# First layer with transposed probabilities and row-wise evidence; squares and feed-forward evacuations on VectorE

## The reference

```
# layer 0, for each of the 16 batches
nx       = layer_norm(x, gamma, beta)                  # 56 x 128
scores   = (nx @ Wq) @ (ctx @ Wk).T * 128 ** -0.5      # 56 x 1500
weights  = softmax(scores)
evidence = weights @ (ctx @ Wv)                        # 56 x 128
combined = [nx, evidence, anchor] -> router, 3 experts, gate -> x = x + delta

# layers 1 to 3: norm -> 16-head attention over the 1500 context rows -> projection
# layers 2 and 3: also self-attention, and h = gelu(norm(x) @ W1 + b1); x = x + h @ W2 + b2
```

## Time and profile before

| what | us |
|---|---|
| median of 3 runs | 1776.51 (1770.99 to 1777.41) |
| profiled execution, its own time | 1769.27 |
| its span, first to last instruction | 1767.5 |
| PE busy | 1562.3 (88%) |
| PEld busy | 996.4 (56%) |
| DVE busy | 1164.7 (66%) |
| ACT busy | 976.2 (55%) |
| POOL busy | 659.8 (37%) |

### The profile page before, as it was taken

How to read it: one execution, slowest core, us unless ns; L and a number is a source line. 1 busy time by engine, 2 the same in 40 slices (tenths; PEclk the granted TensorE clock), 3 DMA queues, 4 the chain that set the end, 5 groups by cost and what they waited for, 6 DMA issues and landing times.

```text
span 1767.5 us, 49986 instructions
## 1 busy us (share of the span) xinstructions
PE 1562.3 (88%) x20479; PEld 996.4 (56%) x20479; DVE 1164.7 (66%) x2425; ACT 976.2 (55%) x1878; POOL 659.8 (37%) x898
## 2 busy tenths in 40 slices
PE   7999977499999998887999999988887999899886
PEld 5667733166666665543566666655443566566554
DVE  3555455577777777366777777764557777777572
ACT  2333323077777677332567776764332677676663
POOL 4000074146666643446366665610332222222110
PEclk9889889599999999798799999997897999999897
DMA  8444214145665544024355655432033466666520
GB/s 240 125 138 145 84 45 95 40 120 133 159 164 152 133 110 116 1 71 109 82 143 152 161 148 147 116 94 47 1 71 93 120 150 160 156 155 146 124 62 6
DMA packets 193275, 199.49 MB, mean 113 GB/s; under 512 B 58949, under 2 KB 182536, under 8 KB 193048
## 3 DMA queue, kind: packets, MB, share of 16 engines
q1 hardware_dynamic: 191464, 195.22, 43.6%
q10 hardware_dynamic: 1008, 1.05, 0.2%
q0 software_dynamic: 576, 0.02, 0.0%
HBM read 114.46 MB, written 72.17 MB: 106 GB/s over the span
## 4 chain that ended last, share of the span: by engine, by line
PE 69%; DVE 13%; ACT 11%; issue 4%; DMA 2%; POOL 1%; SPq 1%; DVEq 0%; ACTq 0%; POOLq 0%
PE PS L1414 14%; PE PS L1242 9%; PE PS L1440 8%; PE PS L1235 7%; PE PS L1388 5%; DVE mx L1881 4%; ACT q_parts L1009 3%; PE PS L1178 3%; PE PS L1188 3%; PE PS L1516 3%; PE PS L1195 3%; ACT v_sb L918 2%; PE PS L1229 2%; PE PS L1089 2%; PE PS L1426 2%
## 5 line engine op out<-in xcount | busy, mean ns | idle before, releaser
L1881 DVE TENSOR_REDUCE mx<-PS 112x1 f32<-112x500 f32 x1152 | 713.5, 672 | 213.3 <-PE PS L1388 211.3
L1009 ACT ACTIVATE q_parts<-PS 125x448 f32<-125x448 f32 x1152 | 562.0, 543 | 159.3 <-PE PS L1440 151.5
L741 POOL CAST k_hi<-k_full 128x500 f16<-128x500 f32 x144 | 89.0, 618 | 631.3 <-issue 556.7
L1440 PEld LDWEIGHTS PS<-q_st,k_st 50*125 50x125 f16 x4608 | 183.5, 137 | 232.1 <-ACT q_parts L1009 162.6
L776 POOL TENSOR_SCALAR cx<-cx,norm_b 125x128 f32<-125x128 f32 x384 | 306.7, 814 | 19.8 <-issue 15.9
L1440 PE MATMUL PS<-q_st,k_st 50*125 50x112 f16 x4608 | 258.7, 233 | 41.5 <-ACT q_parts L1009 32.3
L1414 PE MATMUL PS<-q_parts,v_sb 125*18 125x112 f32 x9216 | 289.0, 268 | 0.0
L1414 PEld LDWEIGHTS PS<-q_parts,v_sb 125*18 125x18 f32 x9216 | 216.3, 100 | 53.2 <-issue 41.3
L1388 PE MATMUL PS<-k_st,q_mx 50*112 50x500 f16 x1080 | 225.2, 384 | 7.6 <-DVE mx L1881 5.2
L743 POOL TENSOR_TENSOR k_lo<-k_full,k_hi 128x500 f16<-128x500 f32 x144 | 163.8, 1138 | 21.1 <-POOL k_hi L741 3.6
L918 ACT ACTIVATE v_sb<-PS 125x512 f32<-125x512 f32 x144 | 86.8, 603 | 98.3 <-PE PS L1242 98.3
(11 more groups left out here) (283 smaller groups left out, 2087.2 us busy)
## 6 DMA issues: line engine op xcount, KB each, us to landing
k_st<-k_dram SPq DMA_DIRECT2D x288, 187.5 KB, 3.6
k_dram<-k_hi SPq DMA_DIRECT2D x288, 125.0 KB, 3.0
cx<-in_ctx SPq DMA_DIRECT2D x40, 672.0 KB
k_dram<-k_lo SPq DMA_DIRECT2D x144, 125.0 KB, 3.1
xT_dram<-k_full SPq DMA_DIRECT2D x16, 750.0 KB, 4.9
cx<-xT_dram SPq DMA_DIRECT2D x32, 375.0 KB
v_sb<-in_ctx SPq DMA_DIRECT2D x8, 672.0 KB
q_st<-q_all SPq DMA_DIRECT2D x48, 99.8 KB
```

The costliest lines, as they stand in the source:

```text
L1009: act.activation(probs[:, c % RING, u * HR:(u + 1) * HR], PS[0:KC, (2 * c + u) % SC_RING, 0:HR], ACT.Exp).then_inc(sem("exp_done"), 1)
L1440: last = mm(PS[0:KC, (2 * c + a) % SC_RING, k * PW:k * PW + PW], k_st[64 * a:64 * a + ROWS, p, k, c * KC:(c + 1) * KC], q_st[64 * a:64 * a ...
L1881: dve.tensor_reduce(mx[:, r, t:t + 1], PS[0:PW, MX_BANK + u % MX_RING, 0:TK], AX.X, ALU.max)\
```

## The change

Layer 0: `turn_probs` becomes 12 true transposes of the raw exponentials against the identity; the diagonal matrix goes. `l0_evidence` holds the turned probabilities (56 columns) as the stationary operand and moves the context chunk (128 columns), so that the evidence comes out with the batch's 56 rows on partitions. VectorE then scales those rows by the reciprocal (`scale_evidence`), and a new transpose on TensorE (`turn_evidence`) turns them for ScalarE's copy. `copy_evidence` moves behind `copy_ctx`. Dense chains: VectorE takes all squares and all first feed-forward evacuations. Cross attention 3: SP's context load moves behind the third `k_out`.

```diff
-            elif kind in ("var", "ffn"):
-                fed = counted("step_fed_act")
...
-            done = counted("step_done_act" if kind == "hid" and u < 2 else "step_done")
+            done = counted("step_done")
...
-                        if layer == 3 and b + 3 < B:
-                            load((b + 3, (b + 3) // 2, 1 - p))
                         k_out(behind, 0)
                         k_in(behind, 0)
                         k_out(behind, 1)
                         k_in(behind, 1)
                         k_out(behind, 2)
+                    if layer == 3 and b + 3 < B:
+                        load((b + 3, (b + 3) // 2, 1 - p))
...
                 l0_exp(b)
+                if b + 1 < B:
+                    copy_ctx(b + 1)
                 if b:
                     copy_evidence(b - 1)
-                if b + 1 < B:
-                    copy_ctx(b + 1)
                 copy_probs(b)
...
-                elif step.kind == "hid" and step.u < 2:
-                    act.wait_ge(sem(step.ready[0]), step.ready[1])
-                    act.activation(hid_h[step.arg], PS[:, bank, 0:HR], ACT.Identity, bias=...)
...
-                if step.kind == "mean" and step.u < 2:
-                    act.wait_ge(sem(step.done[0]), step.done[1])
-                    act.activation(sq_h, cen_h, ACT.Square).then_inc(sem("step_fed_act"), 1)
...
-                pe.wait_ge(sem("diag0_done"), b + 1)
...
-                        last = mm(PS[0:KC, 3 * p + 1 + u, c * T:(c + 1) * T], p0[:, p, k * KC:(k + 1) * KC], diag0[:, p, :],
-                                  start=True, stop=True)
+                        last = pe.transpose(PS[0:KC, 3 * p + 1 + u, c * T:(c + 1) * T], p0[:, p, k * KC:(k + 1) * KC],
+                                            ident[0:T, 0:T])
...
-                    last = mm(PS[:, NT * (b % 2), 0:T], cx0[b % 4][:, c, :], pT0[:, c * T:(c + 1) * T],
+                    last = mm(PS[0:T, 3 * (b % 2), 0:D], pT0[:, c * T:(c + 1) * T], cx0[b % 4][:, c, :],
...
+            def turn_evidence(b):
+                p = b % 2
+                pe.wait_ge(sem("ev_done"), b + 1)
+                pe.transpose(PS[:, 3 * p, 0:T], ev_rows[:, p, :], ident[0:T, 0:T]).then_inc(sem("evT_ready"), 1)
...
                     turn_ctx(b + 1)
+                if b:
+                    turn_evidence(b - 1)
                 turn_probs(b)
...
-            def reciprocal_diagonal(b):
+            def scale_evidence(b):
                 p = b % 2
                 dve.wait_ge(sem("p0_done"), b + 1)
                 dve.reciprocal(rec0[:, p:p + 1], sum0[:, p:p + 1]).then_inc(sem("rec0_done"), 1)
+                dve.wait_ge(sem("ev_ready"), b + 1)
                 dve.wait_ge(sem("rec0_done"), b + 1)
-                dve.tensor_scalar(diag0[:, p, :], ident[0:T, 0:T], rec0[:, p:p + 1], None, ALU.mult)
+                dve.tensor_scalar(ev_rows[:, p, :], PS[0:T, 3 * p, 0:D], rec0[:, p:p + 1], None, ALU.mult)
...
                     row_stats(b, range(5))
-                reciprocal_diagonal(b)
-                if b:
+                    scale_evidence(b - 1)
                     row_stats(b, range(5, C))
                     keep_stats(b)
+            scale_evidence(B - 1)
...
-                    if u > 1:
-                        dve.wait_ge(sem("step_done"), step.done[1])
-                        dve.tensor_tensor(span_of(sq_h, u), cen, cen, ALU.mult).then_inc(sem("step_fed"), 1)
+                    dve.wait_ge(sem("step_done"), step.done[1])
+                    dve.tensor_tensor(span_of(sq_h, u), cen, cen, ALU.mult).then_inc(sem("step_fed"), 1)
```

More of the change, by code:

```diff
@@ L134, in chain_steps @@
 def chain_steps():
-    steps, count = {}, dict(step_ready=0, step_done=0, step_done_act=0, step_fed=0, step_fed_act=0, step_root=0)
+    steps, count = {}, dict(step_ready=0, step_done=0, step_fed=0, step_fed_act=0, step_root=0)
     def counted(name):
@@ L145, in chain_steps @@
             fed = None
-            if kind == "var" and u > 1:
+            if kind == "ffn":
+                fed = counted("step_fed_act")
+            elif kind == "var":
                 fed = counted("step_fed")
-            elif kind in ("var", "ffn"):
-                fed = counted("step_fed_act")
             elif kind in ("spread", "q") or kind == "out" or (kind, arg) == ("hid", 0) or (kind, layer) == ("cq", 1):
@@ L326, in build @@
         max3 = sb("max3", [T, 2, NT])
-        diag0 = sb("diag0", [T, 2, T])
+        ev_rows = sb("ev_rows", [T, 2, D])
         neg0 = sb("neg0", [T, 2])
@@ L875, in copy_evidence @@
             def copy_evidence(b):
-                act.wait_ge(sem("ev_ready"), b + 1)
+                act.wait_ge(sem("evT_ready"), b + 1)
                 act.activation(rows_of(A[6], b), PS[:, NT * (b % 2), 0:T], ACT.Copy).then_inc(sem("evT_done"), 1)
@@ L959, in evacuate @@
                     act.activation(std8[:, 1, 0:pairs_of(step.u)], std8[:, 0, 0:pairs_of(step.u)], ACT.Exp, scale=-0.5).then_inc(sem("step_root"), 1)
-                elif step.kind == "hid" and step.u < 2:
-                    act.wait_ge(sem(step.ready[0]), step.ready[1])
-                    act.activation(hid_h[step.arg], PS[:, bank, 0:HR], ACT.Identity, bias=col(FFN[step.layer][1], step.arg))\
-                       .then_inc(sem("step_done_act"), 1)
             def work_on(step):
-                if step.kind == "mean" and step.u < 2:
-                    act.wait_ge(sem(step.done[0]), step.done[1])
-                    act.activation(sq_h, cen_h, ACT.Square).then_inc(sem("step_fed_act"), 1)
-                elif (step.kind, step.arg) == HIDDEN[-1]:
+                if (step.kind, step.arg) == HIDDEN[-1]:
                     act.wait_ge(sem(step.done[0]), step.done[1])
@@ L1259, in _ @@
             l0_evidence(B - 1)
+            turn_evidence(B - 1)
             pe.wait_ge(sem("w_loaded"), 16 * (len(WEIGHTS) - len(FIRST_WEIGHTS) + 2 * E))
@@ L1699, in reciprocal_diagonal @@
                 dve.reciprocal(rec0[:, p:p + 1], sum0[:, p:p + 1]).then_inc(sem("rec0_done"), 1)
+                dve.wait_ge(sem("ev_ready"), b + 1)
                 dve.wait_ge(sem("rec0_done"), b + 1)
-                dve.tensor_scalar(diag0[:, p, :], ident[0:T, 0:T], rec0[:, p:p + 1], None, ALU.mult)\
-                   .then_inc(sem("diag0_done"), 1)
+                dve.tensor_scalar(ev_rows[:, p, :], PS[0:T, 3 * p, 0:D], rec0[:, p:p + 1], None, ALU.mult)\
+                   .then_inc(sem("ev_done"), 1)
             row_stats(0, range(C))
@@ L1805, in evacuate @@
                 if kind == "hid":
-                    if u > 1:
-                        dve.wait_ge(sem(step.ready[0]), step.ready[1])
-                        dve.tensor_scalar(span_of(hid_h[step.arg], u), src, col(FFN[layer][1], step.arg), None, ALU.add)\
-                           .then_inc(sem("step_done"), 1)
+                    dve.wait_ge(sem(step.ready[0]), step.ready[1])
+                    dve.tensor_scalar(span_of(hid_h[step.arg], u), src, col(FFN[layer][1], step.arg), None, ALU.add)\
+                       .then_inc(sem("step_done"), 1)
                     return
```

## The result

| | median of 6 runs, us |
|---|---|
| before | 1777.42 (1770.99 to 1785.07) |
| after | 1759.26 (1756.67 to 1766.09) |

The ratio is 0.9899 (95% interval 0.9867 to 0.9930): faster by 18 us. Forecast were 1733 us and a gain of 43.5; the direction came true, less than half of the size did, and 1759 lies above the range. The profiled execution took 1759.94 us with a span of 1757.9.

What follows compares the result with a forecast made beforehand. TensorE almost alone was taken to bound layer 0. Batches -26.4, clock -8, start -3.5, end -3.6, dense chains -1 and load -1 sum to -43.5 us: 1776.51 becomes 1733 us, own range 1720 to 1744, 8 in 10 1719 to 1752.

Steps and rivals of the forecast that it cites:

- Turned probabilities, 0.85 us: Layer 0: 12 transposes take 0.85 us a batch, scaled from a 112-column row, in place of 2.75: -1.90 us.
- a transpose's load costs as much as a product's: Rival on layer 0's turned probabilities: 1.38 us in place of 0.85, 8.5 us less gain, 1741 us; chance 0.06.
- half-count bound of 1.38: Layer 0's turned probabilities: half of today's 2.75 us a batch, if only the number of passes falls.
- The load of layer 3, -1: Cross attention 3's context load moved behind the third key write: -1 us, bounds -5 and +9 (third key read queues behind it).
- The evidence, 2.58 us: Layer 0: 24 evidence passes moving 128 columns take 2.58 us a batch against 2.81, -0.23 us.
- What is added: Layer 0's path in each batch: one transpose turning the evidence, 0.07 us, its wait for VectorE covered by context transposes.
- worked sum of 7.92: Layer 0's batch: 2.58 + 2.69 + 2.65 = 7.92 us, taken as 7.95, against 9.98 before.
- The tie of scores and copy: Layer 0: evidence copy ends at 2.67 us, TensorE is ready for scores at 2.69: cost 0, up to 0.5 a batch.
- The clock, -8: Layer 0: two thirds of the 11.8 us lost between batches to a lower clock return, -8 us; bounds 0 and 11.8.
- Start, -3.5: Layer 0's start: the first turned probabilities, at the low clock, take 1.7 us in place of 5.21, -3.5 us.
- End, -3.6: Layer 0's end: the last two batches' turned probabilities and the last evidence shorten, less 0.6 us no longer covered: -3.6 us.
- Dense chains, -1: Squares and first feed-forward evacuations moved from ScalarE to VectorE: -1 us, bounds -8.5 and +9.

Runs made afterwards that it cites:

- e4: The kernel before with only cross attention 3's context load moved behind the third key write: 1784.91 us, ratio 1.0045.
- e6: The kernel before with layer 0's edits alone, and cross attention 3's context load behind the first key write: 1745.13 us, ratio 0.9829.
- e8: The kernel before with layer 0's edits alone, but probabilities turned by 24 ordinary product passes: 1766.87 us in one execution.
- e5: The kernel before with layer 0's edits alone, its probability transposes widened from 125 to 128 columns except the last: 1731.08 us, ratio 0.9755.
- e1: The kernel after with cross attention 3's context load back in front of the first key write: 1748.86 us, ratio 0.9830.
- e9: e5 with the first six probability transposes put in front of the turned context's third tile: 1732.4 us, ratio 0.9751.
- e3: The kernel before with only the squares and first feed-forward evacuations moved to VectorE: 1779.56 us, ratio 1.0014.
- e10: e9 with the evidence's turn and its copy each put in front of the third context tile's: 1727.54 us, ratio 0.9742.

## Why the prediction was wrong in size

The parts run alone add up: layer 0 -1.88%, chains +0.14%, load +0.45%, together -1.29%, which is -23 us. Measured were -18. The intervals (0.3% or so on each) cover the 5 us between; that the moved load costs more beside the other edits than alone isn't excluded. The last stage of the profiled executions, before, after, e4 and e6, with the columns of the earlier trace rows:

```profile
1354.00:1767.00 413.00, 364.53 (x5716) 235.62 (x5713) 291.29 (x544) 257.74 (x507) 73.22 (x84) 0.93 0.48 116
```

```profile
1328.00:1757.00 429.00, 373.07 (x5716) 240.81 (x5716) 294.20 (x549) 255.30 (x502) 73.36 (x84) 0.91 0.47 111
```

```profile
1361.00:1782.00 421.00, 365.02 (x5714) 235.80 (x5713) 290.76 (x544) 257.94 (x507) 73.23 (x84) 0.93 0.48 114
```

```profile
1325.00:1742.00 417.00, 371.99 (x5714) 240.03 (x5713) 291.37 (x544) 257.74 (x507) 73.22 (x84) 0.91 0.49 115
```

TensorE is idle for 48.5, 55.9, 56.0 and 45.0 us of them. So of the 15.8 us by which the stage grew, 7.5 are waiting, as in e4, and 8.5 are the same work at a lower clock: the last batch alone took 26.5 us against 19.4, with the clock at 0.70 from 1676 to 1710. e4 has the late load and not the lower clock, e6 the lower clock and not the late load, so no run ties the one to the other. What brought the clock down in this stage is open.

By the steps of the prediction:

- **Turned probabilities, 0.85 us: the first step that failed.** It measured 1.31. The row that I scaled was one of 112 columns, and 125 don't follow it; my rival "a transpose's load costs as much as a product's", with its half-count bound of 1.38 and a chance of 0.06, was the truth for 125 columns (0.115 us a load before, 0.109 now, and 0.109 in e8's products, 2.62 us for 24). I kept the count of columns as a factor, but the step from 112 to 125 wasn't a matter of amount: 128 columns cost 0.066 each (e5). 0.46 x 16 = 7.4 us. The Trainium skill's price by the columns alone ("TensorE: Matmul & The Clock Gate", LDWEIGHTS) gave an estimate of 1.25 us, near the 1.31. For 128 columns the estimate by it is 1.28, and the trace has 0.79, so there the trace doesn't agree with the page.
- **The load of layer 3, -1: the largest error of a single step, +8** (e4, e1), near the upper bound of 9 but by another wait than the one named. The prediction asked who waits for the key reads that stand around the load; it didn't ask who waits for the load itself, and by how much of a lead it had been covered.
- **The evidence, 2.58 us:** 2.62. **What is added:** the turn of the evidence 0.20, not 0.07, and the first four context transposes 0.59 in place of 0.45, as their first load hides less behind the evidence: it starts 0.07 us before the evidence ends, against 0.27 before. With the 0.46 and 0.04 this makes the 0.76 by which 8.68 misses the worked sum of 7.92. The batches gave 13 x 1.30 = 16.9 us for 26.4.
- **The tie of scores and copy: right to put at 0**, as TensorE came later than worked out; e9 shows the tie where TensorE comes earlier. (The exponentials end at 138.8 by the earlier trace rows, not at 139.0; nothing hangs on it.)
- **The clock, -8:** the full 11.8. **Start, -3.5:** 2.0, for the reason of the first step, twice as long at the low clock (2.70 us). **End, -3.6:** from the evidence of batch 13 to L1266 22.0 us before and 17.38 now, -4.6, and L1266 itself at a higher clock, 2.35 us for 4.21, -1.9.
- Together 16.9 + 11.8 + 2.0 + 4.6 + 1.9 = 37.1 us at the end of layer 0. Of these 3.6 were gone by the first maximum: the 24 products right behind the layer's end took longer. The chain before, and then after:

```profile
221.97 9.30 PE PS L1089 x24
```

```profile
184.84 12.18 PE PS L1082 x24
```

  The granted clock from there to the first maximum was 0.78 after (180 to 303 us) and 0.80 before (217 to 336). That I had not looked for, and it isn't a price of the change: e6, with the same layer 0, has these 24 products in 9.30 us and its first maximum at 298.18. So the 33.5 us carry a few us of a clock that differs from kernel to kernel.
- **Dense chains, -1:** +2.5 in the middle of e3's interval, which takes in 0; the batches show 2.4, all from squares.

## What to carry to other kernels

When a transfer is moved in a queue, ask first who waits for that transfer and how long its lead was; here the price was there, 8 us, and not with its neighbours. Where a transpose's loads bind, try other column counts than the natural one (128 for 125 here), as the price wasn't proportional; for a product's loads (186 and 192 ns) the same padding showed nothing to gain. Before filling a gap, add up the engine's own work around it: in e10 it was 7.98 us, with no gap left to fill. And run a change's parts alone: here +0.45%, +0.14% and -1.88% looked like one edit of -1%.

## What the hardware showed that I had not expected

An f32 transpose's load of 125 columns took 186 ns, one of 128 columns 138 ns, and in a row they came every 0.109 and 0.066 us. The 112-column one of the earlier trace rows comes every 0.064. Whether it is the odd count or that 125 is no multiple of four or sixteen wasn't tried. A product's load of 128 columns took 192 ns, so it is not the count alone.

The clock fell to half for parts of layer 0 in all four kernels that turn the probabilities by 24 product passes (before, e3, e4, e8), out of stretches in which TensorE was busy nearly throughout (10.75 of 11.00 us from 150 to 161 in e8, then 0.54 from 161 to 168), and in none of the eight that do it by 12 transposes (117.48 of 121.00 us busy at 1.00 from 49 to 170 in after). By its busy share alone the one stretch looks like the other. What in the 24 passes does it, their number, their loads or the product itself, isn't shown.
